# Eight small tables picked by a one-hot product instead of gathers, in a DLRM tower

## The reference

```python
e = jnp.stack([tbl_0[ids[:, 0]], tbl_1[ids[:, 1]], ..., tbl_31[ids[:, 31]]], axis=1)   # 512 x 32 x 32
x0, prev = e, e
for W in (filter_0, filter_1):                 # 1024 x 128 and 4096 x 128
    z = jnp.einsum('bhd,bmd->bhmd', x0, prev)  # all pairs of fields
    cur = relu(jnp.einsum('bpd,pn->bnd', z.reshape(b, h * m, d), W[0]))
    prev = cur; outs.append(cur)
z = jnp.sum(jnp.concatenate(outs, axis=1), axis=-1)          # 512 x 256
h = jnp.maximum(jnp.concatenate([z, dense_ctx], axis=1) @ W_top1 + b_top1, 0.0)
h = jnp.maximum(h @ W_top2 + b_top2, 0.0)
y = h @ W_top3
```

## Time and profile before

| | |
|---|---|
| Profiled execution | 882.07 us, span 880.3 us |
| TensorE (PE) busy | 831.2 us (94%) |
| DVE busy | 773.2 us (88%) |
| ACT busy | 725.0 us (82%) |
| POOL busy | 657.8 us (75%) |
| Mean granted TensorE clock | 0.998 of full speed |

### The profile page before, as it was taken

How to read it: one execution, slowest core, us unless ns; L and a number is a source line. 1 busy time by engine, 2 the same in 40 slices (tenths; PEclk the granted TensorE clock), 3 DMA queues, 4 the chain that set the end, 5 groups by cost and what they waited for, 6 DMA issues and landing times.

```text
span 880.3 us, 17918 instructions
## 1 busy us (share of the span) xinstructions
PE 831.2 (94%) x3608; PEld 668.5 (76%) x3608; DVE 773.2 (88%) x2425; ACT 725.0 (82%) x2425; POOL 657.8 (75%) x642
## 2 busy tenths in 40 slices
PE   0189999999999999999999999999999999999998
PEld 0168888888888888888888878888788888888875
DVE  4158999999999999999999999999999999999995
ACT  2248889988888898988888889888888898888873
POOL 7767898878888888878888878866666766666652
PEclk9999999999999999999999999999999999999999
DMA  7035776667667766676677666766676666766540
GB/s 197 12 88 129 175 167 151 134 137 164 152 149 170 167 149 145 135 155 158 146 165 175 153 145 127 153 158 144 159 172 149 146 128 142 164 144 153 97 92 5
DMA packets 78618, 124.38 MB, mean 141 GB/s; under 512 B 34177, under 2 KB 36993, under 8 KB 78594
## 3 DMA queue, kind: packets, MB, share of 16 engines
q0 software_dynamic: 22240, 68.17, 41.0%
q1 hardware_dynamic: 56354, 55.96, 21.3%
HBM read 54.99 MB, written 3.05 MB: 66 GB/s over the span
## 4 chain that ended last, share of the span: by engine, by line
PE 71%; POOL 16%; DMA 6%; issue 3%; DVE 3%; ACT 0%; DVEq 0%; POOLq 0%
PE bank L864 60%; PE bank L804 9%; DMA parts<-parts 5%; POOL rows L347 4%; POOL pair_low L382 4%; POOL w_sb L366 2%; POOL parts L359 2%; POOL w_sb L373 2%; DVE acc L765 2%; POOL rows L397 2%; POOL half L366 1%; PE bank L870 1%; PE bank L896 1%; PE bank L835 1%; DVE acc L775 0%
## 5 line engine op out<-in xcount | busy, mean ns | idle before, releaser
L545 ACT ACTIVATE parts<-bank,x 128x128 f32<-128x128 f32 x2048 | 588.2, 379 | 97.2 <-PE bank L864 88.7
L765 DVE SCALAR_TENSOR_TENSOR acc<-bank,x,acc 128x128 f32<-128x128 f32 x1792 | 484.4, 342 | 43.8 <-PE bank L864 43.8
L864 PE MATMUL bank<-w_high,cur_high 128*128 128x512 f32 x1024 | 402.3, 393 | 1.6 <-ACT cur_high L492 0.7
L864 PE MATMUL bank<-w_low,cur_high 128*128 128x512 f32 x1024 | 399.3, 390 | 0.0
L864 PE MATMUL bank<-w_high,cur_low 128*128 128x512 f32 x992 | 388.1, 391 | 0.0
L864 PEld LDWEIGHTS bank<-w_high,cur_high 128*128 128x128 f32 x1024 | 192.2, 188 | 49.6 <-DVE acc L765 7.3
L864 PEld LDWEIGHTS bank<-w_low,cur_high 128*128 128x128 f32 x1024 | 192.3, 188 | 40.1
L864 PEld LDWEIGHTS bank<-w_high,cur_low 128*128 128x128 f32 x992 | 186.2, 188 | 40.5
L382 POOL TENSOR_TENSOR pair_low<-pair,pair_high 128x512 fp32r<-128x512 f32 x124 | 158.7, 1299 | 22.1 <-ACT pair_high L481 21.5
L366 POOL TENSOR_TENSOR half<-parts 128x512 f32<-128x512 f32 x64 | 82.8, 1294 | 116.7 <-DMA parts<-parts 116.6
L397 POOL DMA_INDIRECT rows<-table_dram,ids_sb x96 | 97.8, 1019 | 30.8 <-issue 30.3
(11 more groups left out here) (95 smaller groups left out, 555.0 us busy)
## 6 DMA issues: line engine op xcount, KB each, us to landing
parts<-parts POOLq DMA_DIRECT2D x126, 512.0 KB, 6.6
shifts<-x_scratch SPq DMA_DIRECT2D x155, 256.0 KB
x<-x_scratch SPq DMA_DIRECT2D x31, 256.0 KB, 2.9
x_scratch<-turned SPq DMA_DIRECT2D x124, 24.0 KB, 1.8
rows<-table_dram,ids_sb POOLq DMA_INDIRECT x128, 2.5
wt<-w_top_dram SPq DMA_DIRECT2D x2, 512.0 KB, 9.2
w_sb<-w_ab_dram SPq DMA_DIRECT2D x1, 256.0 KB
w_t<-w_ba_dram SPq DMA_DIRECT2D x1, 256.0 KB
```

The costliest lines, as they stand in the source:

```text
L545: ins = nc.scalar.activation(parts[q][ab][:, at:at + N2], act_bank[ab][:, i * N2:(i + 1) * N2], ACT.Copy, scale=x0[u][:, h, 2 * q + ab:2 * ...
L765: nc.vector.scalar_tensor_tensor(out=dst, in0=dve_bank[e % 2 * 2 + ab][:, i * N2:(i + 1) * N2], scalar=x0[u][:, h, 2 * q + ab:2 * q + ab + ...
L864: return nc.tensor.matmul(dst[:], cur_half[u][:, cols], w1_half[:, fields], **flags)
```

## The change

The eight 1000-row tables are no longer gathered for block 0; the other three blocks still gather all 32. Instead each of the eight is loaded whole: 125 partitions of 8 rows (1 KB). DVE compares the sample's id with the first row of each partition and gets a one-hot matrix (partition x sample) per table; a float32 matmul with the table brings the 8 rows of the right partition to each sample (`picked_bank`), and another with the first-row numbers brings that partition's first row (`base_bank`). The difference to the sample's own id says which of the 8 rows is wanted; a mask and a sum over 8 leave one row in `rows`.

Beside it: the second filter's halves are made in eight pieces of 512 columns; TensorE no longer waits for `w1_low` before `keep_busy` but just before the first chunk; 24 gathers remain, of which fields 17 to 23 (without 22) come last; the turn for chunk 1 stands behind the spreads on DVE and behind the first spread on ACT; and `dve_pair` waits for `loaded` and `x4_ready` once per chunk instead of five times.

```diff
+W1_PIECES = 8
+FIRST_COPIES = 4
+SMALL_PAIRS = [(9, 12), (22, 26), (27, 28), (30, 31)]
+SMALL = [f for fields in SMALL_PAIRS for f in fields]
+EACH_ROWS = 8
+SMALL_PARTS = 125
+GATHERED = [f for f in range(F) if f not in SMALL]
+LAST_FIELDS = (17, 24)
...
+        ids_wide = parts[0][0][:, 512:512 + len(SMALL) * P].bitcast(INT32)
+        small_table = [parts[1][0][:, i * EACH_ROWS * D:(i + 1) * EACH_ROWS * D] for i in range(len(SMALL))]
+        wide_bank, picked_bank, base_bank = bank[0:2], bank[2:6], cur_bank
...
             sp.dma_start(ids_sb[:], ids.rearrange("(k p) f -> p k f", p=P)).then_inc(ids_in, 16)
+            sp.dma_start(ids_wide, bass.AP(small_ids.tensor, small_ids.offset,
+                                           [[0, P], [1, len(SMALL) * P]])).then_inc(small_ids_in, 16)
+            sp.dma_start(first_row[:], small_rows).then_inc(small_ids_in, 16)
+            sp.dma_start(own_ids[:], small_own).then_inc(small_ids_in, 16)
...
             sp.dma_start(parity_sb[:], parity).then_inc(w0_in, 16)
+            for f, table in zip(SMALL, small_table):
+                sp.dma_start(table[0:SMALL_PARTS, :],
+                             tables[f].rearrange("(p k) d -> p (k d)", k=EACH_ROWS)).then_inc(small_in, 16)
             sp.dma_start(w1_sb[:], w1.rearrange("(h m) n -> m h n", h=F)).then_inc(w1_in, 16)
...
-            for f in range(F):
+            for f in sorted(GATHERED, key=lambda f: LAST_FIELDS[0] <= f < LAST_FIELDS[1]):
                 nc.gpsimd.indirect_dma_start(
...
+            pool.wait_ge(small_done, len(SMALL_PAIRS))
             nc.gpsimd.memset(mark[:], 0.0).then_inc(rows_ready, 1)
...
             act.wait_ge(w1_in, 16)
-            nc.scalar.copy(w1_high[:], w1_sb[:].rearrange("m h n -> m (h n)")).then_inc(w1_high_done, 1)
+            for piece in range(W1_PIECES):
+                nc.scalar.copy(w1_high[:, piece * 512:(piece + 1) * 512],
+                               w1_flat[:, piece * 512:(piece + 1) * 512]).then_inc(w1_high_done, 1)
...
+            act.wait_ge(first_fields_ready, FIRST_COPIES)
+            act_spread(2)
+            act.wait_ge(small_done, len(SMALL_PAIRS))
             act_turn_waits(act, 1)
             act_turn(act, 1)
-            act.wait_ge(first_fields_ready, 3)
-            act_spread(2)
...
-                dve.wait_ge(loaded, c * (LOADS * 16))
-                dve.wait_ge(x4_ready, c)
+                if step == PAIR_ORDER[0]:
+                    dve.wait_ge(loaded, c * (LOADS * 16))
+                    dve.wait_ge(x4_ready, c)
...
+            dve.wait_ge(small_ids_in, 3 * 16)
+            for i in range(2):
+                nc.vector.tensor_copy(wide_bank[i][:], ids_wide[:, i * 512:(i + 1) * 512]).then_inc(wide_copied, 1)
+            nc.vector.tensor_copy(own_row[:], own_ids[:]).then_inc(own_step, 1)
...
-            dve.wait_ge(w1_high_done, 1)
-            nc.vector.tensor_tensor(w1_low[:], w1_sb[:].rearrange("m h n -> m (h n)"), w1_high[:].bitcast(FP32),
-                                    ALU.subtract).then_inc(w1_low_done, 1)
+            dve.wait_ge(wide_copied, 2)
+            for i in range(2):
+                nc.vector.tensor_scalar(at_least[i], wide_bank[i][:], first_row[:, 0:1], None,
+                                        ALU.is_ge).then_inc(compared, 1)
+            for i in range(2):
+                dve.wait_ge(compared, i + 1)
+                nc.vector.scalar_tensor_tensor(out=one_hot[i], in0=wide_bank[i][:], scalar=first_row[:, 1:2],
+                                               in1=at_least[i], op0=ALU.is_lt, op1=ALU.mult).then_inc(one_hot_done, 1)
             nc.vector.memset(wt1_dense[:].bitcast(FP32), 0.0).then_inc(dense_zeroed, 1)
             nc.vector.memset(dense_sb[:].bitcast(FP32), 0.0).then_inc(dense_zeroed, 1)
+            for piece in range(W1_PIECES):
+                dve.wait_ge(w1_high_done, piece + 1)
+                at = slice(piece * 512, (piece + 1) * 512)
+                nc.vector.tensor_tensor(w1_low[:, at], w1_flat[:, at], w1_high[:, at].bitcast(FP32),
+                                        ALU.subtract).then_inc(w1_low_done, 1)
+            dve.wait_ge(picked, len(SMALL))
...
+            for i in range(len(SMALL_PAIRS)):
+                nc.vector.tensor_tensor(
+                    masked[i].rearrange("p (r d) -> p r d", d=D), picked_bank[i][:].rearrange("p (r d) -> p r d", d=D),
...
+                nc.vector.tensor_reduce(rows[:, 0, first:second + 1:second - first, :],
+                                        masked[i].rearrange("p (j r d) -> p j d r", j=2, d=D),
+                                        mybir.AxisListType.X, ALU.add).then_inc(small_done, 1)
             dve.wait_ge(dense_high, 8)
...
-            dve_turn(dve, 1)
-            dve.wait_ge(first_fields_ready, 3)
+            dve.wait_ge(first_fields_ready, FIRST_COPIES)
             for step in (-1, 1, 0):
                 nc.vector.tensor_copy(spread_out(step), first_fields(step)).then_inc(dve_wide, 1)
+            dve_turn(dve, 1)
...
             pe.wait_ge(w0_done, 4)
-            pe.wait_ge(w1_low_done, 1)
-
-            pe.wait_ge(first_gathered[0], (F - LAST_TABLES) * 16)
+            pe.wait_ge(small_in, len(SMALL) * 16)
+            for i in range(len(SMALL)):
+                pe.wait_ge(one_hot_done, i // 4 + 1)
...
+                nc.tensor.matmul(base_bank[:, i:i + 1], rows_of_sample, first_row[0:SMALL_PARTS, 0:1], start=True, stop=True)
+                nc.tensor.matmul(picked_bank[i // 2][:, half_bank], rows_of_sample, small_table[i][0:SMALL_PARTS, :],
+                                 start=True, stop=True).then_inc(picked, 1)
+            pe.wait_ge(w1_high_done, 1)
+            pe.wait_ge(first_gathered[0], (len(GATHERED) - LAST_TABLES) * 16)
             keep_busy(WARM_UP, warm_bank)
...
+            pe.wait_ge(w1_low_done, W1_PIECES)
```

More of the change, by code:

```diff
@@ L183, in dlrm_tower @@
         w1_in = sem("w1_in")
+        small_ids_in = sem("small_ids_in")
+        small_in = sem("small_in")
+        wide_copied = sem("wide_copied")
+        compared = sem("compared")
+        one_hot_done = sem("one_hot_done")
+        picked = sem("picked")
+        own_step = sem("own_step")
+        mask_done = sem("mask_done")
+        small_done = sem("small_done")
         w0_in = sem("w0_in")
@@ L817, in keep_busy @@
             for _ in range(count):
-                nc.tensor.matmul(to[:], w1_high[:, 0:P], w1_high[:, 0:COLS], start=True, stop=True)
+                nc.tensor.matmul(to[:], w1_high[:, 0:P], w1_high[:, 0:512], start=True, stop=True)
         @block.tensor
```

43 lines of the change are left out of this document (36 added, 7 removed).

## The result

The changed kernel takes 876.6 us, median of 7 runs (875.19 to 878.21), beside 882.1 us for the kernel before (7 runs); ratio 0.9936, 95% interval 0.9923 to 0.9949. It is faster by 5.5 us where 8.7 were forecast. The profiled execution took 876.62 us, its span is 874.8 us (before 880.3).

What follows compares the result with a forecast made beforehand. POOL's gathers were taken to bound the 50.1 us ahead of TensorE's matmuls. 882.07 - 9.2 (earlier transposes) + 0.1 (given back) + 0.4 (clock) = 873.4 us; own range 871.5 to 876.5, with rivals 868.2 to 877.5.

Steps and rivals of the forecast that it cites:

- rival 2: Table and id loads: queue slower still, 17.6 GB/s per engine, ids at half rate; filter at 28.5, 877.3 us; chance 0.10.
- The gathers: POOL ahead of the transposes: with 24 gathers, last issued at 34.3 and landed at 36.8, 11.8 us earlier.
- The first (all 16 engines): Table loads: spread over all 16 DMA engines, filter lands at 18.3, gathers bound again; 870.0 us; chance 0.27.
- The third: Loads on SP's queue: 128 reads of the same 4 KB one behind the other, slower than before, 901.8 us; chance 0.05.
- 1.7 + 1.0 us: POOL's gathers: 1.7 us for five gathers that meet DVE's pieces, 1.0 us for the smaller delays of before.
- The second filter: Its landing behind the new loads: 14.07 + 1.4 for wide ids + 9.1 for tables on five engines = 24.6.
- From the filter to the transposes: DVE's pieces to 30.8, pick to 36.8, dense subtractions to 39.6; transposes at 40.9 instead of 50.1, 9.2 us earlier.
- TensorE's picks: 8 float32 products of 256 columns, 4 us or 8 at half clock, done by 25, hidden before DVE asks at 30.8.
- The clock: TensorE stands still about 7 us before the transposes instead of 3.4: 0.4 us more at half clock.
- What is given back: Chunk 1's shifts leave 1.55 us later relative to TensorE as the turn moves behind the spreads: 0.1 us, at most 0.6.

Runs made afterwards that it cites:

- the run with even tables: The changed kernel with each table loaded as 112 and 13 partitions, two loads instead of one: 872.8 us, ratio 0.9885.
- the pieces alone: The kernel before, all 32 gathers kept, with only the second filter's halves made in eight pieces: 879.25 us, ratio 0.9964.
- the one piece: The changed kernel with the second filter's halves made in one piece again, tables and 24 gathers left: 878.44 us, ratio 0.9966.
- the run with repeated ids: The changed kernel with the wide ids read from a DRAM tensor that holds them 128 times: 877.44 us, ratio 0.994.
- dense subtractions later: The changed kernel with the four dense subtractions moved behind `dve_low16(0)`, no longer ahead of the copies of gathered rows: 872.47 us, ratio 0.9883.
- 38 warm matmuls: The changed kernel with 38 instead of 16 warm matmuls on TensorE ahead of the transposes: 878.41 us, ratio 0.9947.
- moving the turn back: The changed kernel with the turn ahead of the spreads on DVE and ACT, as before the change: 876.03 us, ratio 0.9943.

## Why the prediction was right, and where it was short

**The order of the causes held.** The time lies inside the whole range (868.2 to 877.5) but just outside the forecast's own (871.5 to 876.5): the room that took it in had been left for rival 2, which did not come about. The gathers ceased to be the bound, the second filter's landing became it, DVE was busy from there to the copies, and the picks of TensorE, `keep_busy`, ACT's casts and the one-hot stayed hidden. The three rivals fell. The first (all 16 engines) needs other loads: the run with even tables shows what it would have been, 872.8, not 870.0. The second came to nearly its number for the wrong reason: its place was a filter at 28.5, and the ids' single address costs nothing in the time. The third needed a filter that lands behind 33.8.

**The gathers.** Last issue forecast at 34.3, measured 32.95. The 1.7 + 1.0 us set down for delays were 1.2 (32.95 less the start at 3.24 less 28.5); of the gathers that met pieces one was held, by 0.17 us (27.80). That the 4.56 us of the earlier trace rows were a wait for DVE is shown by the pieces alone and, once more, by the one piece. It did not matter for the sum.

**The second filter: the term that was short by 2.1 us.** Forecast 24.6 (14.07 + 1.4 + 9.1), measured 26.75. The landings tell where it went. ACT's first cast waits for the last helper of the first filter, before and after:

```profile
6.06 0.30 ACT L501 CAST w_half_r<-w_half_sb 128x128 fp32r<-128x128 f32 x1 [4.04 <-DMA parity_sb<-parity_dram]
```
```profile
9.59 0.30 ACT L540 CAST w_half_r<-w_half_sb 128x128 fp32r<-128x128 f32 x1 [7.56 <-DMA parity_sb<-parity_dram]
```

The three id loads pushed the helpers back by 3.5 us, where 1.4 were put: that is the 2.1 us. The tables land 9.9 us behind the helpers (19.46; 9.1 put), and the filter 7.3 us behind the tables, where it came 8.0 behind the helpers before; these two nearly cancel. Why the id loads cost so much is open: SP issues the last helper 1.4 us later (4.64 instead of 3.23), and the run with repeated ids did not bring the helpers back. The forecast also left out SP's own time: eleven loads more ahead of the filter, each 0.3 to 1.1 us of issuing, so that SP issued it at 10.88 instead of 3.88. In the kernel after that is hidden, as far as the landings tell, since the tables landed only at 19.46; with even tables it shows. The tables' uneven shares were real: they land at least 5.5 us later than in even ones, and 15.85 us pass from the filter's issue to its landing instead of 10.2 to 10.5. The Trainium skill (page "DMA: Bandwidth & Descriptors", section "Why a DMA increments its semaphore by 16 and not by 1") has the rule that agrees, the largest number up to 16 that divides the slowest dimension, five for 125 and 16 for 112; no view here shows the single engines.

**From the filter to the transposes.** The pieces took 4.95 us until the pick (32.35 - 27.40), 0.65 less than the 5.6 forecast. The pick took 6.86 instead of 6.0, because a reduction of 512 elements to 64 takes 1.0 us, not 0.70 (3.98 for four). Dense subtractions 2.87 (2.8). Together with the filter: 43.17 instead of 40.9, and 2.3 of the 3.2 us that are missing.

**TensorE's picks** were forecast at 4 us, 8 at half clock; they take 1.28 us per table, 10.2 in all, 19.46 to about 30. That was hidden with only 2 us to spare before DVE asks at 32.35. The clock column shows 1.00 there, but for want of a record: the trace's clock records begin at 37.88. The warm matmuls behind the picks start 0.43 us apart up to 37.9 and 0.23 us apart from there on, so TensorE was most likely at the lower level until then, and the picks with it.

**The clock.** +0.4 forecast; the way from the transposes to the first second-layer matmul is 9.67 us, 8.98 before: +0.7. The sign and the cause were right. That the half clock costs 2.2 us there in all was not seen: 7.47 and 7.41 us with dense subtractions later and with 38 warm matmuls.

**What is given back.** 0.1 forecast, as DVE's late shifts in chunk 0; measured 0.74. This step named the wrong cause. The shifts of chunk 0 were later (a wait of 1.33 us instead of 0.53), and moving the turn back cured that without curing the loss. In the kernels with a larger lead that cause does cost something, in chunk 0. In the kernel after the loss is the collision of accumulating transfers with shift reads in chunks 2 to 4. It was in no part of the prediction, which read the chain as staying on TensorE from the transposes on, though the chain of before goes over six such transfers from 376.76 us on, and took everything behind the transposes as a shifted copy of before. Why SP's reads come closer to the pairs there is open: in the kernel before they were issued 3.2 us behind the start of the turn's writes (117.74 to 120.94), in the kernel after 4.5 us (111.38 to 115.90), since SP waited 2.5 us instead of 1.2 for those writes to land. What holds the writes was not tried.

Sum of the parts: 2.3 + 0.3 + 0.6 = 3.2 us between 8.7 and 5.5.

## What to carry to other kernels

When a load is put ahead of a critical one, count three things: its bytes, how evenly its rows can be dealt out, and the issuing engine's time for each load; here even shares brought the second filter 4.1 us earlier (22.67 instead of 26.75), with the issuing time as the next bound, and splitting 125 rows into 112 and 13 gave 0.5% (872.8 against 876.6). Work for a waiting engine that is not needed yet (the dense subtractions) belongs behind the point that everything waits for, and pays twice if it shortens an idle stretch of TensorE. And a lead at the start is not the gain at the end: two streams of transfers that hardly met can meet more closely once the phase moves; follow the lead along the kernel, event by event, before adding more of it.

## What the runs showed of the hardware that was not expected

- Reads of 64 columns of DRAM rows in place of 512 leave the accumulating transfers beside them undisturbed: the first of a pair lands 4.7 us behind its issue at 3.4 to 4.2 us behind the first read, where full reads make it 5.9 to 7.0 at 3.4 to 3.8 us and 7.0 to 8.2 at 2.5 to 3.1.
- A load in which 128 partitions read the same 4 KB of DRAM comes over 1 us later than one in which they read different ones (DVE's first cast at 6.8 to 7.4 us and at 5.59), with no gain in the time (876.6 and 877.4 us).
- A clock column of 1.00 can mean that nothing is recorded yet. The warm matmuls of 512 columns start 0.43 us apart and then, from one to the next, 0.23: behind the 13th in the kernel after, behind the 8th with 26 of them. The clock records of the two traces begin just there (37.88 and 34.94 us), with 1.00.
- A gather is held until 0.82 and 0.83 us behind the end of DVE's subtraction in progress, and eight subtractions of an eighth of the size hold one by at most 0.51 us (1.45 us instead of 0.94).
